# Products of zeros ahead of the first work on TensorE, three register loads moved into the first block, and a send of rows one turn earlier

## The chip, the cores and the metric

The kernel runs on one core of one Trainium2 chip. The metric is the device time of one execution in microseconds; of several runs the median is given. The five engines are TensorE (PE in the profile, its weight loads PEld), VectorE (DVE), ScalarE (ACT), GpSimd (POOL) and SyncE (SP, which issues most DMAs). Each engine executes its own instructions in order, and they wait for each other by semaphores.

## The reference

One layer of a transformer over x of 4 batches x 512 rows x 128 channels, float32:

```
x = x + LN2( attention(LN1(layernorm(x))) @ Wo )       # 16 query heads of 64, ONE key/value head
x = x + MoE(layernorm(x))
MoE: probs = softmax(x @ gate_w.T); the two best of 8 experts, shares normalised to sum 1
     for an expert: hact = up * gelu(gate), (gate, up) = x @ gate_up_w.T (512 each); out = hact @ down_w.T
```

## The kernel before

**First block, attention.** A unit is 8 heads of one batch; there are 8 units. `attention_schedule` writes one list of steps (kind, unit, number), sorted by hand-set slots, and each engine walks the same list and does its part of each step. For batch 0 the steps are: STAT0 and APPLY0 (layernorm), XT (four transposes, L1091), K (three products of split float32 operands, L1069 to L1071), Q (the same three lines, two heads at a time; ScalarE and VectorE then split the result into `q_hl`, VectorE at L974), MAX (one product per 128 queries of a head, L1121, and VectorE's row maximum, L985), SHIFT (the maxima transposed, L1128, copied by ScalarE, and sent by DMA into row 64 of `q_hm`), EXP (two products into `s_ps`, L1150 and L1152, and ScalarE's exp), V (twelve small products, L1069 to L1071), PV (L1166), SUM (L741), and NORM and OUT per head pair. For the first 12 MAX steps the slots lie ahead of the first EXP. The chain is long there: TensorE waits for layernorm, for the split of x on ScalarE and VectorE, for the split of the query weights on GpSimd (`wql`, L870), and for every second row maximum.

While batches 1 to 3 are in attention, the steps AFTER_STEPS of the batch before run in between: second layernorms, the routing (CHOOSE), PLACE, and LIST, which writes into `tile_at` which expert each tile of 128 rows has and where its rows begin. Rows are sent to their places in `sorted_rows` by indirect DMAs on GpSimd (`send_rows`, L464), eight for a batch.

**Second block, experts.** There are 39 tiles. The turn of tile k is on TensorE: turn_in(k+1) (a transpose, L1450), the register load of tile k's expert number (L1499), gate(k) and up(k) (L1461 in plain float32 for the first six tiles, L1462 to L1464 for the others), turn_hidden(k-1) (L1473), down(k-2) (L1486). ScalarE does the gelu and copies, VectorE the product of up and gelu (L1336) and `weigh` (L1345), GpSimd sends each tile's weighted rows to `parts` (L1299). The block opens with tiles 0 to 2 written out by hand: `turn_in(0)`, three register loads, eight waits for the weights of the experts, `gate(0)`, `up(0)`, and then the last unit's NORM and OUT steps in between. In this stretch ScalarE makes the high parts `wh` of the weights (L1382), and VectorE and GpSimd the low parts `wl` (L1256). GpSimd starts the block with the eight row sends of batch 2, then makes eight pieces of `wl`, then the power of the last batch's layernorm (L441). The steps of the last batch are spread over the turns by the table `BETWEEN` (PLACE in turn 9, LIST3 in turn 12). Its eight row sends follow from turn `SEND_AT` on, two, one, two, one, two per turn; while they last, GpSimd sends no results. GpSimd begins turn k once `weigh(k-3)` is done. Tiles 17 to 38 are loaded by SyncE once the last list is written and all rows are sent. The results are read back and added at the end.

## Time and profile before

| | us |
|---|---|
| median of 3 runs (lowest, highest) | 633.98 (633.31, 635.54) |
| the profiled execution: its time | 634.79 |
| its span from first to last instruction | 633.0 |
| TensorE busy | 575.8 (91%) |
| VectorE, ScalarE, GpSimd busy | 422.4, 303.7, 391.3 |

The sums that follow are made on the profiled execution's clock, on which 1.8 us lie around the span. Times of rows are from the start of the span. The matmul records' ends are modelled and reach into the next matmul, so the distance from start to start tells the rate.

### The profile page before, as it was taken

How to read it: one execution, taken by the hardware profiler on the slowest of the kernel's cores; microseconds unless marked ns; L12 is line 12 of the kernel's file. 1: busy time of each engine (PE TensorE's matmuls, PEld its weight loads, DVE VectorE, ACT ScalarE, POOL GpSimd, SP SyncE). 2: the span in 40 equal slices, each digit the busy share in tenths (PEclk: the TensorE clock that was granted, in tenths of full speed). 3: DMA queues.
4: the chain of work that ended last, by engine and by line, in shares of the span. 5: the costliest groups of instructions: out<-in, count | busy, mean ns of one | idle time of the engine just before them, and what ended most of it. 6: DMA issues, size and time to landing. Idle time of an engine off the chain costs nothing. (4 is left out here: it accounts for less than half of the span.)

```text
span 633.0 us, 8708 instructions
## 1 busy us (share of the span) xinstructions
PE 575.8 (91%) x2559; PEld 324.4 (51%) x2559; DVE 422.4 (67%) x815; ACT 303.7 (48%) x570; POOL 391.3 (62%) x319
## 2 busy tenths in 40 slices
PE   2799999999999999979999989899997989899990
PEld 1354454444554454445544544444442567788880
DVE  3777558658847978686587767977485868344433
ACT  2235655445545554354556434355544654455540
POOL 4338686658668855598597556959755934355330
PEclk9889999999999999789999978999998999999995
DMA  6121011010101100061000000000006200231005
GB/s 173 47 88 69 2 68 69 0 69 0 70 16 53 69 1 1 5 250 47 1 1 1 2 1 15 17 6 0 10 1 167 64 22 27 53 97 36 21 14 199
DMA packets 23980, 29.28 MB, mean 46 GB/s; under 512 B 4403, under 2 KB 14901, under 8 KB 23936
## 3 DMA queue, kind: packets, MB, share of 16 engines
q1 hardware_dynamic: 21664, 24.50, 11.9%
q0 software_dynamic: 2272, 4.24, 2.0%
q8 instruction: 23, 0.38, 0.3%
q14 instruction: 21, 0.17, 0.1%
HBM read 13.73 MB, written 15.32 MB: 46 GB/s over the span
## 5 line engine op out<-in xcount | busy, mean ns | idle before, releaser
L1059 ACT ACTIVATE prob<-s_ps 128x512 f32<-128x512 f32 x256 | 150.6, 598 | 191.5 <-PE s_ps L1152 189.5
L985 DVE TENSOR_REDUCE rowmax<-max_ps 128x1 f32<-128x512 f32 x256 | 173.1, 685 | 90.1 <-PE max_ps L1121 88.4
L922 POOL TENSOR_TENSOR fold<-prob 128x1024 f32<-128x1024 f32 x63 | 149.6, 2374 | 96.7 <-ACT prob L1059 96.2
L1166 PE MATMUL pv_ps<-prob,v 128*64 128x512 f32 x512 | 140.4, 628 | 0.0
L1150 PE MATMUL s_ps<-q_hl,khh 128*128 128x512 f32 x256 | 119.3, 466 | 1.5 <-DMA q_hm<-mrow 0.9
L1121 PE MATMUL max_ps<-khh,q_hl 128*128 128x512 f32 x256 | 106.0, 422 | 9.0 <-DVE q_hl L974 4.4
L1152 PE MATMUL s_ps<-q_hm,kly 65*128 65x512 f32 x256 | 102.9, 402 | 0.0
L1150 PEld LDWEIGHTS s_ps<-q_hl,khh 128*128 128x128 f32 x256 | 49.3, 193 | 81.7 <-ACT prob L1059 58.1
L928 POOL TENSOR_TENSOR psums<-fold 128x512 f32<-128x512 f32 x63 | 81.3, 1290 | 4.9
L1121 PEld LDWEIGHTS max_ps<-khh,q_hl 128*128 128x128 f32 x256 | 50.4, 197 | 30.0 <-DVE rowmax L985 10.4
L1152 PEld LDWEIGHTS s_ps<-q_hm,kly 65*128 65x128 f32 x256 | 49.4, 193 | 9.1 <-issue 3.3
L1166 PEld LDWEIGHTS pv_ps<-prob,v 128*64 128x64 f32 x512 | 25.8, 137 | 46.5 <-issue 35.3
L974 DVE TENSOR_TENSOR q_hl<-q_ps,q_hl 64x512 fp32r<-64x512 f32 x64 | 44.1, 689 | 6.5 <-ACT q_hl L1041 5.2
L1336 DVE TENSOR_TENSOR ha<-up_ps,gl 128x512 f32<-128x512 f32 x39 | 26.9, 690 | 30.6 <-PE up_ps L1464 23.5
L464 POOL DMA_INDIRECT sorted_rows<-xr,place_i x32 | 32.6, 1020 | 23.5 <-issue 11.9
L1486 PE MATMUL sum_ps<-wd,ht 128*128 x312 | 41.8, 277 | 2.6 <-DVE raw L1345 2.4
L907 POOL TENSOR_SCALAR q_hm<-q_hl 64x1024 fp32r<-64x1024 f32 x32 | 33.3, 1039 | 12.5 <-ACT q_hl L1041 12.5
L1041 ACT ACTIVATE q_hl<-q_ps 64x512 fp32r<-64x512 f32 x64 | 37.6, 587 | 6.5 <-PE q_ps L1071 5.7
L1299 POOL DMA_INDIRECT parts<-raw,psums x22 | 21.3, 970 | 30.4 <-DVE raw L1345 27.7
L1486 PEld LDWEIGHTS sum_ps<-wd,ht 128*128 128x128 f32 x312 | 37.9, 192 | 3.8 <-issue 3.8
L709 DVE TENSOR_TENSOR ao<-sum_ps,raw 128x512 f32<-128x512 f32 x32 | 22.0, 688 | 21.7 <-PE sum_ps L751 21.6
L761 PE MATMUL y_ps<-ao,wof 128*128 128x512 f32 x64 | 34.8, 628 | 0.0
(218 smaller groups left out, 769.9 us busy)
## 6 DMA issues: line engine op xcount, KB each, us to landing
sorted_rows<-raw_w SPq DMA_DIRECT2D x36, 260.0 KB, 2.6
raw_w<-in_gate_upT SPq DMA_DIRECT2D x8, 512.0 KB, 7.6
wd<-in_downT SPq DMA_DIRECT2D x8, 256.0 KB, 4.2
raw_w<-parts SPq DMA_DIRECT2D x8, 256.0 KB, 4.0
psums<-sorted_rows SPq DMA_DIRECT2D x22, 65.0 KB, 1.8
x<-in_x SPq DMA_DIRECT2D x4, 256.0 KB, 5.3
out<-x SPq DMA_DIRECT2D x4, 256.0 KB, 2.7
xs_first<-sorted_rows SPq DMA_DIRECT2D x15, 65.0 KB, 1.9
```

The source lines that it names most:

```text
L761: nc.tensor.matmul(y_ps[:, :], wof[:, c, :], ao[:, k % 2, :], start=c == 0, stop=c == PAIRS - 1).then_inc(out_mm, 1)
L922: nc.gpsimd.tensor_tensor(fold[:, :, :], prob[:, head % 4, 0:2, :], prob[:, head % 4, 2:4, :], ALU.add).then_inc(prob_folded, 1)
L928: nc.gpsimd.tensor_tensor(psums[:, head % SUM_SLOTS, :], fold[:, 0, :], fold[:, 1, :], ALU.add).then_inc(head_sum, 1)
L974: nc.vector.tensor_tensor(q_hl[DH:P, h % Q_SLOTS, :], q_ps[DH * hd:DH * hd + DH, :], q_hl[0:DH, h % Q_SLOTS, :].bitcast(F32), ALU.subtract ...
L985: nc.vector.tensor_reduce(rowmax[:, group % 2, it, i:i + 1], max_ps[:, k % 2, :], AX_X, ALU.max).then_inc(max_done, 1)
L1041: nc.scalar.activation(q_hl[0:DH, (2 * k + hd) % Q_SLOTS, :], q_ps[DH * hd:DH * hd + DH, :], ACT.Copy).then_inc(q_hi, 1)
L1059: nc.scalar.activation(prob[:, head % 4, jt, :], s_ps[:, k % 2, :], ACT.Exp, scale=SCALE).then_inc(exp_done, 1)
L1121: nc.tensor.matmul(max_ps[:, k % 2, :], q_hl[:, k // JT % Q_SLOTS, it * P:(it + 1) * P], khh[:, b % 2, :], start=True, stop=True).then_inc ...
L1150: nc.tensor.matmul(s_ps[:, k % 2, :], khh[:, b % 2, keys], q_hl[:, slot, :], start=True, stop=False)
L1152: nc.tensor.matmul(s_ps[:, k % 2, :], kly[0:DH + 1, b % 2, keys], q_hm[0:DH + 1, slot, :], start=False, stop=True).then_inc(score_mm, 1)
L1166: last = nc.tensor.matmul(pv_ps[DH * hd:DH * hd + DH, :], v[:, b % 2, jt, :], prob[:, head % 4, jt, :], start=(jt == 0), stop=(jt == JT - 1))
L1486: last = nc.tensor.matmul(down_ps[:, :], ht[:, k % 2, c * P:(c + 1) * P], wd[:, weights(k, DN, c * P, P)], start=c == 0, stop=c == FC - 1)
```

## The change

It has three parts. (1) TensorE multiplies a tile of zeros (`idle_rows`, slot 9 of `q_hm`, cleared by GpSimd at the start) into `y_ps`, which nothing reads: 20 times ahead of everything, 8 times ahead of K, 5 ahead of the first MAX, once ahead of each of MAX 2 to 11, 3 times ahead of the first EXP and 3 ahead of V. (2) The three register loads of tiles 0 to 2 stand in the first block, ahead of the last SUM. (3) `SEND_AT` is 9 where it was 10, so that the last batch's row sends begin in the turn of PLACE.

```diff
+BUSY = {"start": 20, "K": 8, "MAX": 5, "EXP": 3, "V": 3, "rows": 1}
+OPEN = 3
...
+        idle_set = sem("idle_set")
...
+        tile_expert = []
+        def load_expert(pe, k):
+            tile_expert.append(pe.value_load(tile_at[0:1, 0, k:k + 1], min_val=0, max_val=E - 1))
...
+            idle_rows = q_hm[:, Q_SLOTS - 1, :]
...
             def _(pool):
+                nc.gpsimd.memset(idle_rows.bitcast(F32), 0.0).then_inc(idle_set, 1)
                 nc.gpsimd.memset(minus_half[:, :], -0.5).then_inc(half_set, 1)
...
+                def keep_busy(times):
+                    for _ in range(times):
+                        nc.tensor.matmul(y_ps[:, :], idle_rows[:, 0:P], idle_rows, start=True, stop=True)
+                pe.wait_ge(idle_set, 1)
+                keep_busy(BUSY["start"])
                 pe.wait_ge(consts_in, 96)
                 in_bank = None
                 for kind, u, a in steps:
                     b = u // 2
+                    if u == 0 and a == 0 and kind in BUSY:
+                        keep_busy(BUSY[kind])
...
                         if it == 0:
                             pe.wait_ge(q_lo, u * UH + i + 1)
+                        if 2 <= k < 12:
+                            keep_busy(BUSY["rows"])
                         if k >= 2:
                             pe.wait_ge(max_done, k - 1)
...
+                    if (kind, u, a) == ("SUM", last_unit, 1):
+                        pe.wait_ge(tiles_ready, 1)
+                        for k in range(OPEN):
+                            load_expert(pe, k)
                     tail_tensor(pe, kind, u, a)
...
-            SEND_AT = 10
+            SEND_AT = 9
...
-            assert SEND_AT > BETWEEN["PLACE"] and EOW >= TOP_K * TPB + 4
+            assert SEND_AT >= BETWEEN["PLACE"] and EOW >= TOP_K * TPB + 4
...
-                tile_expert = []
                 turn_in(0)
-                for k in range(OPEN):
-                    expert(k)
```

How TensorE's first instructions stand, before and then with the change (the lines of the changed kernel lie 18 to 33 lines further down; L1102 is a product of zeros):

```order
L1091 MATMUL q_ps<-ident,x 128x128 [waits xn_ready,consts_in]
L1091 MATMUL q_ps<-ident,x 128x128 x3
L1069 MATMUL pv_ps<-xh,wkh 128x512 [waits wkv_split,xl_ready]
L1070 MATMUL pv_ps<-xh,wkl 128x512
L1071 MATMUL pv_ps<-xl,wkh 128x512
L1069 MATMUL q_ps<-xh,wqh 128x512 [waits xl_ready,wq_split,xnT_sb]
```

```order
L1102 MATMUL y_ps<-q_hm 128x512 [waits idle_set]
L1102 MATMUL y_ps<-q_hm 128x512 x19
L1119 MATMUL q_ps<-ident,x 128x128 [waits xn_ready,consts_in]
L1119 MATMUL q_ps<-ident,x 128x128 x3
L1102 MATMUL y_ps<-q_hm 128x512 x8
L1087 MATMUL pv_ps<-xh,wkh 128x512 [waits wkv_split,xl_ready]
L1088 MATMUL pv_ps<-xh,wkl 128x512
L1089 MATMUL pv_ps<-xl,wkh 128x512
L1087 MATMUL q_ps<-xh,wqh 128x512 [waits xl_ready,wq_split,xnT_sb]
L1088 MATMUL q_ps<-xh,wql 128x512
L1089 MATMUL q_ps<-xl,wqh 128x512
L1102 MATMUL y_ps<-q_hm 128x512 x5
```

The products of zeros stand ahead of the waits, so they run while the awaited data is made.

TensorE from the last PV of the first block over the block's end (the branches) to the first gate, before and then with the change; TENSOR_LOAD reads a register from `tile_at`:

```order
L1166 MATMUL pv_ps<-prob,v 64x512 [waits exp_done]
L1166 MATMUL pv_ps<-prob,v 64x512
L741 MATMUL sum_ps<-psums,sumsel 32x512 [waits vec_sum,head_sum]
L741 MATMUL sum_ps<-psums,sumsel 32x512 x3
L770 UNCONDITIONAL_BRANCH
L1438 UNCONDITIONAL_BRANCH [waits barrier_Pool_Activation_PE_DVE_SP_release]
L1450 MATMUL pv_ps<-ident,xs_early 128x128 [waits xs_in0,raw_ready]
L1499 TENSOR_LOAD tile_at
L1499 ISA x2
```

```order
L1196 MATMUL pv_ps<-prob,v 64x512 [waits exp_done]
L1196 MATMUL pv_ps<-prob,v 64x512
L661 TENSOR_LOAD tile_at [waits tiles_ready]
L661 ISA x2
L661 TENSOR_LOAD tile_at
L661 ISA x2
L661 TENSOR_LOAD tile_at
L661 ISA x2
L755 MATMUL sum_ps<-psums,sumsel 32x512 [waits vec_sum,head_sum]
L755 MATMUL sum_ps<-psums,sumsel 32x512 x3
L784 UNCONDITIONAL_BRANCH
```

The loads, three before as after, moved from behind the first transpose of the second block to ahead of the last SUM of the first.

GpSimd in turns 9 to 14, before and then with the change (L457 and L465 write the rows' ids, L464 and L472 send rows, L1299 and L1332 send results):

```order
L457 COPY xr<-ids 128x8 [waits rows_sent,eow_ready]
L1299 DMA parts<-raw,xs_first 4096x128 [waits x3_copied,eow_ready,place_ready,pool_own]
L464 DMA sorted_rows<-xr,place_i 18432x130 [waits eow_ready]
L464 DMA sorted_rows<-xr,place_i 18432x130
L464 DMA sorted_rows<-xr,place_i 18432x130 [waits eow_ready] x2
L464 DMA sorted_rows<-xr,place_i 18432x130
L464 DMA sorted_rows<-xr,place_i 18432x130 [waits eow_ready] x2
```

```order
L465 COPY xr<-ids 128x8 [waits rows_sent,eow_ready]
L472 DMA sorted_rows<-xr,place_i 18432x130 [waits x3_copied,place_ready,pool_own]
L472 DMA sorted_rows<-xr,place_i 18432x130
L472 DMA sorted_rows<-xr,place_i 18432x130 [waits eow_ready] x2
L472 DMA sorted_rows<-xr,place_i 18432x130
L472 DMA sorted_rows<-xr,place_i 18432x130 [waits eow_ready] x2
L472 DMA sorted_rows<-xr,place_i 18432x130
L1332 DMA parts<-raw,xs_first 4096x128 [waits eow_ready] x11
```

One send of results went from ahead of the eight row sends to behind them, and each row send waits for the `weigh` of one tile less.

## Rows read from the trace of the kernel before

**Rows 1.** The page of the profile, part 2 (40 equal slices): the granted clock.

```profile
PEclk9889999999999999789999978999998999999995
```

**Rows 2.** Windows: start:end, length, each engine's busy us, granted clock, DMA share, GB/s.

```profile
25.10:28.50 3.40, 3.19 (x9) 1.97 (x10) 2.52 (x5) 0.59 (x1) 0.00 (x0) 0.50 0.00 0
42.10:45.50 3.40, 3.40 (x9) 1.04 (x8) 1.29 (x2) 0.60 (x1) 0.00 (x0) 0.51 0.00 0
0.00:42.10 42.10, 24.00 (x78) 14.52 (x79) 25.85 (x44) 13.79 (x24) 17.30 (x33) 0.96 0.36 116
482.50:485.90 3.40, 3.28 (x4) 1.40 (x5) 1.21 (x2) 0.00 (x0) 2.78 (x3) 0.50 0.81 230
```

**Rows 3.** Timeline, TensorE, 8 to 31 us: start, us, engine, line, operation, idle before.

```profile
8.74 1.09 PE L1091 MATMUL q_ps<-ident,x 128*128 128x128 f32 x4 [8.74 <-ACT x L360]
...
12.57 0.80 PE L1069 MATMUL pv_ps<-xh,wkh 128*128 128x512 f32 x1 [2.74 <-DVE xl L963]
...
19.07 0.63 PE L1069 MATMUL q_ps<-xh,wqh 128*128 128x512 f32 x1
19.50 0.63 PE L1070 MATMUL q_ps<-xh,wql 128*128 128x512 f32 x1
...
28.63 0.39 PE L1070 MATMUL q_ps<-xh,wql 128*128 128x512 f32 x1
28.86 0.40 PE L1071 MATMUL q_ps<-xl,wqh 128*128 128x512 f32 x1
...
30.15 0.47 PE L1150 MATMUL s_ps<-q_hl,khh 128*128 128x512 f32 x1 [0.90 <-DMA q_hm<-mrow]
```

**Rows 4.** Timeline, GpSimd and VectorE, 12 to 32 us.

```profile
12.06 1.58 POOL L870 TENSOR_TENSOR wql<-prob,wqh 128x512 fp32r<-128x512 f32 x1
...
29.91 1.41 DVE L974 TENSOR_TENSOR q_hl<-q_ps,q_hl 64x512 fp32r<-64x512 f32 x2 [0.71 <-ACT q_hl L1041]
```

**Rows 5.** Timeline, TensorE, at the value projection of the first batch.

```profile
40.09 0.30 PE L1069 MATMUL q_ps<-wvh,xh 128*128 128x64 f32 x1 [0.94 <-DVE q_hl L974]
```

**Rows 6.** Timeline, ScalarE and TensorE, around the end of the first block.

```profile
475.04 0.60 ACT L1059 ACTIVATE prob<-s_ps 128x512 f32<-128x512 f32 x1 [1.02 <-PE s_ps L1152]
...
477.66 1.06 PE L741 MATMUL sum_ps<-psums,sumsel 128*32 128x512 f32 x8
...
482.62 2.07 PE L1461 MATMUL gate_ps<-raw_w,xe 128*128 x2 [2.52 <-issue]
...
486.04 0.27 PE L1450 MATMUL pv_ps<-ident,xs_early 128*128 128x128 f32 x1
```

**Rows 7.** Line L1499, TensorE's sequencer: ns min/median/max, first and last start.

```profile
L1499 PEldq TENSOR_LOAD <-tile_at x3: 311/312/489, 479.8 to 481.4; - x3
...
L1499 PEldq TENSOR_LOAD <-tile_at x1: 303/303/303, 549.4 to 549.4; - x1
```

**Rows 8.** Timeline, GpSimd and VectorE, 490 to 507 us.

```profile
490.69 1.41 POOL L1256 TENSOR_TENSOR wl<-raw_w,wh 128x512 fp32r<-128x512 f32 x1 [0.83 <-ACT wh L1382]
...
503.98 1.04 POOL L441 TENSOR_TENSOR rstd<-var_eps,minus_half 128x4 f32<-128x4 f32 x1 [0.18 <-DVE var_eps L480]
...
506.02 1.13 DVE L500 SCALAR_TENSOR_TENSOR x<-z,rstd,x 128x128 f32<-128x128 f32 x4
```

**Rows 9.** Timeline, all engines, 528 to 549 us.

```profile
528.66 0.98 POOL L1299 DMA_INDIRECT parts<-raw,xs_first  x1 [3.50 <-DVE raw L1345]
...
536.56 0.34 DVE L1345 TENSOR_SCALAR raw<-sum_ps,xs_first 128x128 f32<-128x128 f32 x1
...
542.14 0.97 POOL L464 DMA_INDIRECT sorted_rows<-xr,place_i  x1 [0.30 <-issue]
...
544.28 1.06 PE L1486 MATMUL sum_ps<-wd,ht 128*128 x8
...
547.23 0.30 PE L1450 MATMUL pv_ps<-ident,psums 128*128 128x128 f32 x1 [1.89 <-DMA psums<-sorted_rows]
...
548.11 0.49 PE L1462 MATMUL gate_ps<-wh,xeh 128*128 x1 [0.58 <-issue]
```

More of the change, by code:

```diff
@@ L1215, in bass_preln_mqa_moe_kernel @@
             parts_in = [sem(f"parts_in{b}") for b in range(NB)]
-            OPEN = 3
             BETWEEN = {"YT": 3, "YSTAT": 3, "YADD": 4, "XSTAT": 4, "XNORM": 5, "X3T": 6, "LOGIT": 6, "CHOOSE0": 6, "CHOOSE1": 7,
@@ L1495, in between_step @@
                     after_tensor(pe, kind, LB, bank)
-                def expert(k):
-                    tile_expert.append(pe.value_load(tile_at[0:1, 0, k:k + 1], min_val=0, max_val=E - 1))
                 def gate(k):
@@ L1550, in _ @@
                             pe.wait_ge(tiles_ready, 2 if k < FIRST_TILES else 3)
-                        expert(k)
+                        load_expert(pe, k)
                         if k == RAW_TILES:
```

## The prediction, made before the changed kernel ran

> **What bounds the kernel now.** TensorE is busy for 575.8 of 633.0 us, so I looked first for the stretches in which it is not, or in which it works at half rate. The windows say where: up to 42.1 us it is busy for only 24.0, so 18.1 us are idle [rows 2]. The timeline of the same stretch says that work, too, is slow there: at 19 us two products of 512 columns start 0.43 us apart, at 28.6 us 0.23 apart [rows 3]. The first is the 1.2 GHz level of the clock and the second 2.4 GHz. The granted clock is not written down for the time before its first change, so the page and the windows print 1.00 there; the distances in the timeline are what counts. Two more falls to 0.50 come at 25.1 and 42.1, 3.4 us each, both behind stretches in which TensorE waited [rows 2]. From about 45 us on TensorE is the bound, and what it reaches earlier there stays. The digits of the page show later falls (slices 17 and 18, 24 and 25, 31) [rows 1]; only the last is touched by the change.
>
> The second place is the change of blocks. The last SUM starts at 477.66, and the first gate at 482.62, after 2.52 us for which nothing is named but "issue" [rows 6]; the row of line L1499 says what it is, three register loads, the first at 479.8 and the third at 481.4 [rows 7]. Gate and up then run at the clock of 0.50 [rows 2], and the next transpose starts at 486.04 [rows 6].
>
> The third is tile 17. TensorE's down product of turn 15 starts at 544.28 and ends at 545.34, the transpose of tile 17 waits 1.89 us for a DMA and starts at 547.23, and the gate only at 548.11, because the register load stands behind the transpose [rows 9].
>
> **Part 1, zeros at the start.** Added are one clearing on GpSimd (about 0.5 us at a time when it waits for statistics) and 49 products. At half rate they are 49 x 0.43 = 21 us, at full rate 49 x 0.23 = 11 us, against 18.1 us of idle time [rows 2, 3], so the clock decides. The 20 opening ones start near 1.4 us; at full rate throughout they end at 6.0, at half rate at 10.0. I take the middle, 8, for a clock that rises among them; the transposes could start at 8.74 before [rows 3], so nothing is lost, and 1.3 is if it does not rise.
>
> What the chain up to the first score product at 30.15 [rows 3] then saves, each at full instead of half rate: the four transposes 1.09 to about 0.6, 0.5; K's three products 3 x 0.20 = 0.6, of which 0.3 is lost, since Q must wait for GpSimd's `wql`, which ends at 13.64 [rows 4]; the first Q 0.6; the second Q 0.6; the transposes of SHIFT about 0.45; and five MAX products that stand alone between two row maxima, 0.80 each before as the lone product at 12.57, 0.47 as the lone one at 30.15 [rows 3], 1.5 in all (estimate from these two). That is 3.95; VectorE's own pace takes some back, as its row maxima follow each other without a gap once TensorE is fast, and I take 3.4. The check is VectorE's third split at 29.91 [rows 4], which should come near 26.5. The zeros ahead of MAX and EXP lie in waits (EXP waited 0.90 for the DMA [rows 3], three zeros are 0.7).
>
> Then V: 0.94 us of waiting [rows 5], into which three zeros go (0.7). Behind it came the fall at 42.1, in which TensorE was busy throughout [rows 2]; at half rate it lost half of 3.4, 1.7. With the zeros I think the fall is avoided more often than not, but falls in between are possible too: I take 1.0, with bounds of -0.5 and 1.7. The Trainium skill, "TensorE: Matmul & The Clock Gate", Part 1, says that the default state is throttled and that activity releases the throttle; by that rule alone the zeros pay the whole 1.7, and the trace agrees in that every fall stands behind waits. Neither says that operands of zeros count as activity, which is a rival below.
>
> **Part 2, the loads.** They leave the front of the second block, but do not vanish. In the old place their starts are 0.8 us apart [rows 7], three are 2.4. In the new place they stand behind the last PV, whose wait is over when the last exp ends, at 475.64 [rows 6]. The sequencer runs ahead of the array: the load at 549.4 is one of a turn whose gate comes more than one us later and costs nothing [rows 7, 9]. So loads run from 475.7 to 478.1, and SUM starts there and not at 477.66: 0.4 later. If the sequencer could not run ahead, they would start as the PV products end, at 477.7, and cost 2.4. I take 0.4, by the nearer row. The Trainium skill, "DMA: Bandwidth & Descriptors", table of latencies, gives about 0.6 us as the floor of such a load; by it three end at 477.5 and SUM is not delayed; the row shows 0.8, and the row decides.
>
> Everything of the second block moves with SUM, by 0.4 later. What does its front gain? The gate starts some 2.0 earlier (of the 2.52, part is the waits for the weights, which stay), and if the clock then holds, gate and up take 2.0 and not 3.4: 3.5 in all by the transpose at 486.04, 2.0 if it falls again. But TensorE is not alone here. GpSimd has eight sends first and then eight pieces of `wl` until 503.8, and only then the power of the layernorm at 503.98 [rows 8]. Its slack is what counts: it waited 0.83 for ScalarE at 490.69, of which 0.6 can go; 0.18 at 503.98; and its power ended at 505.02, 1.0 before VectorE used it at 506.02 [rows 8]. So VectorE comes there at most 0.6 + 0.18 + 1.0 = 1.8 earlier, and the split of tile 6, the product of tile 5 and `weigh(2)` are queued behind it on VectorE, which TensorE's down(3) waits for. Gain of part 2: the smaller of 1.8 and the front, less 0.4, is 1.4.
>
> **Part 3, the row sends.** A send and the idle time after it are 0.97 + 0.30 = 1.27. The first goes where a send of results stood, 528.66. The last two now wait for `weigh` of tile 10, over at 536.90, and not of tile 11; with about 0.8 to the issue (estimate) the last is issued at 539.0 instead of 542.14. From that issue to the transpose of tile 17 were 5.1 us [rows 9], so its rows are there at 544.1, 1.1 before they are due at 545.2. The wait goes wholly, and the load behind it hides again: 548.11 - 545.3 = 2.8. Moved past it is one send of results; `eow` has 16 buffers and no more than six results are behind, so nothing waits for it.
>
> **The sum.** 3.4 + 1.0 + 1.4 + 2.8 = 8.6, from 634.79: 626.2. The profiled execution is 0.8 above the median of the runs, so by the median it could be 625.4; I say 626.0.
>
> **Rivals.** (a) *The clock falls once more among the zeros.* Between the eight zeros ahead of K and the first MAX, TensorE works for K and Q only, and GpSimd's 13.64 [rows 4] holds it. A fall there or in V costs 1.7 and more of the chain: the start gives 2.0 and not 4.4, 628.6. For it: the falls at 25.1 and 42.1 came behind waits of the same size. (b) *GpSimd does not bind in the second block*: its pieces of `wl` may get shorter when VectorE's move away from them. Then the front's 3.5 - 0.4 remain, 624.5. (c) *The loads wait for the array*: 2.0 more, 628.2. (d) *The row sends do not free tile 17*, because the list or a send comes later than I think: 2.8 less, 629.0. This is also the case that part 3 does not do what it says. (e) *Zeros do not raise the clock*, and lie on the path at 0.43 each. Price: 20 from 1.4 end at 10.0 against 8.74, 1.3; 8 are 3.4 against 2.74 of waiting [rows 3], 0.7; 5 ahead of MAX 0.7; ten single ones 4.3 against some 2.7 of waits, 1.6; EXP and V 0.3 each; 4.9 in all. With parts 2 and 3 at 4.2 this ends at 635.5, slower than before; it decides from 4.2 us of uncovered zeros on. Against it: the rows before show a clock that followed how busy TensorE was, and nothing in them ties it to values; nothing in them excludes it either.
>
> **How the numbers follow.** Noise first: the three runs spread over 0.35%, and 0.3% (1.9 us) is about what can be told from no change. Chances: the forecast 0.60 (its own range 624.3 to 628), (a) 0.17, (b) 0.08, (c) 0.04, (d) 0.06, (e) 0.05. The range reaches to (a) to (d) with their spread: 623.3 to 630. All cases but (e) are faster by more than 1.9; with something for a pile-up of (a), (c) and (d), faster is 0.92, same 0.05, slower 0.03.
>
> **What the changed profile would show.** Right: products of zeros 0.23 apart before 8.7; the first score product near 26.8; clock at 1.00 from 42 to 45 of the old count; SUM 0.4 later than the last exp allows; the first gate within 2 us of the block's start; the power on GpSimd right behind its last `wl` piece with VectorE waiting for it; tile 17's transpose without a wait for DMA. Wrong: zeros 0.43 apart beyond 9 us, a fall between 9 and 30, an idle TensorE ahead of SUM of over 1 us, or a wait for `psums` rows at tile 17.

## The result, and the profile after

The changed kernel takes 628.81 us in the median of 20 executions (623.05 to 634.88), the kernel before 634.84 in the same sitting (20 executions, 631.76 to 636.23): a ratio of 0.9896 [0.9874, 0.9917]. It is 6.0 us faster, and its median lies 2.8 above the forecast of 626.0. Its executions lie much further apart than those of before, and time goes with the mean granted clock of an execution: 0.985 at 623.05, 0.965 at 634.88. Medians are over all executions; ratios leave out those more than 1.5% above the fastest of their kernel (two of the 20 here). In a later sitting the same program was measured again beside the kernel before, and the ratio was 0.9979 [0.9952, 1.0006]. The two intervals do not touch, and the second just includes no change. So the changed kernel is faster by 1.0% in one sitting and by 0.2% in the other, and the experiments below are compared by what their traces show stage by stage first, and by ratios second.

The profiled execution has a span of 629.1 (time 631.12) against 633.0. The table cuts it at five starts on TensorE: the 17th score product of a `u`, the last SUM, and the transposes that turn in tiles 6, 16 and 38.

| stage | before | after | change | forecast |
|---|---|---|---|---|
| start to the 17th score product | 58.82 | 55.46 | -3.36 | -4.4 |
| from there to the last SUM | 418.84 | 413.40 | -5.44 | +0.4 |
| SUM to tile 6's transpose | 28.90 | 36.15 | +7.25 | -1.8 |
| tile 6 to tile 16 | 35.77 | 35.77 | 0.0 | 0 |
| tile 16 to tile 38 | 65.20 | 62.32 | -2.88 | -2.8 |
| tile 38 to the end | 25.42 | 26.06 | +0.64 | 0 |

Two lines agree with the forecast and two do not at all: the attention lost 5.4 us for which no term stood in the sum, and the opening of the second block grew by 7.3 where it should have shrunk.

The granted clock of after, from the page, beside [rows 1]:

```profile
PEclk9999999999999999889999999999998799999995
```

Slices 24 and 25, around 373 us, read 7 and 8 before and read 9 now; so do the second and the third, which read 8. The windows of two falls that after has of its own (columns as in [rows 2]):

```profile
14.80:18.20 3.40, 3.40 (x9) 2.33 (x7) 1.95 (x3) 1.19 (x2) 1.84 (x3) 0.50 0.00 0
489.30:496.10 6.80, 3.45 (x10) 2.31 (x11) 6.16 (x5) 0.60 (x1) 1.61 (x2) 0.50 0.16 39
```

The start, timeline of TensorE in after, beside [rows 3]:

```profile
3.68 4.04 PE L1102 MATMUL y_ps<-q_hm 128*128 128x512 f32 x15
8.52 0.63 PE L1119 MATMUL q_ps<-ident,x 128*128 128x128 f32 x4 [0.81 <-ACT x L368]
...
12.18 0.50 PE L1087 MATMUL pv_ps<-xh,wkh 128*128 128x512 f32 x1 [1.18 <-DVE xl L981]
...
14.06 0.47 PE L1087 MATMUL q_ps<-xh,wqh 128*128 128x512 f32 x1 [0.92 <-issue]
...
14.83 2.34 PE L1102 MATMUL y_ps<-q_hm 128*128 128x512 f32 x5
...
28.50 0.47 PE L1180 MATMUL s_ps<-q_hl,khh 128*128 128x512 f32 x1 [0.36 <-DMA q_hm<-mrow]
```

The zeros do raise the clock: fifteen in 4.04 us, the four transposes in 0.63 instead of 1.09, K at the full rate. But then the clock falls: the five zeros at 14.83 take 2.34, which is a distance of 0.43, and the window above says 0.50. And the first query product starts at 14.06, no earlier than in the trace of before (14.02), because it waits for GpSimd, whose last piece of `wq` ends at 13.96, 0.3 later than in [rows 4]. The piece ahead of it took 1.06 where it took 0.62 before; VectorE's split of `x`, which is earlier now, ran beside it until 12.12. First TensorE in before, then GpSimd in after:

```profile
14.02 0.63 PE L1069 MATMUL q_ps<-xh,wqh 128*128 128x512 f32 x1
...
11.54 1.06 POOL L887 TENSOR_SCALAR wqh<-prob 128x512 fp32r<-128x512 f32 x1
12.68 1.28 POOL L888 TENSOR_TENSOR wql<-prob,wqh 128x512 fp32r<-128x512 f32 x1
```

The first score product starts 1.65 us earlier, not 3.4.

The opening of the second block, timeline of TensorE in after, beside [rows 6]:

```profile
468.86 1.06 PE L755 MATMUL sum_ps<-psums,sumsel 128*32 128x512 f32 x8 [0.25 <-issue]
470.95 0.33 PE L1483 MATMUL pv_ps<-ident,xs_early 128*128 128x128 f32 x1 [1.03 <-ACT raw L733]
471.84 1.75 PE L1494 MATMUL gate_ps<-raw_w,xe 128*128 x2 [0.56 <-ACT xe L1424]
...
475.09 0.42 PE L1483 MATMUL pv_ps<-ident,xs_early 128*128 128x128 f32 x1
```

From SUM to the second transpose it is 6.23 us, 8.38 before: the loads are gone from there, and the gain of 2.15 is there although the clock falls again. What took it back, and 7 us more, stands a little later. GpSimd, VectorE and TensorE, timelines of after:

```profile
481.05 9.87 POOL L1289 TENSOR_TENSOR wl<-raw_w,wh 128x512 fp32r<-128x512 f32 x8
...
481.73 0.69 DVE L723 TENSOR_TENSOR ao<-sum_ps,raw 128x512 f32<-128x512 f32 x1
482.34 9.65 DVE L1289 TENSOR_TENSOR wl<-raw_w,wh 128x1024 fp32r<-128x1024 f32 x1
491.92 0.68 DVE L723 TENSOR_TENSOR ao<-sum_ps,raw 128x512 f32<-128x512 f32 x1
...
492.65 2.07 PE L775 MATMUL y_ps<-ao,wof 128*128 128x512 f32 x2 [7.71 <-DVE ao L723]
```

VectorE's second piece of `wl` is recorded with 9.65 us. The same instruction took 1.30 in the kernel before, timeline of VectorE:

```profile
493.15 1.30 DVE L1256 TENSOR_TENSOR wl<-raw_w,wh 128x1024 fp32r<-128x1024 f32 x1
...
496.93 4.48 DVE L1256 TENSOR_TENSOR wl<-raw_w,wh 128x1024 fp32r<-128x1024 f32 x2 [1.26 <-ACT wh L1382]
```

So three of VectorE's four pieces ran while GpSimd's eight were under way (490.69 to 503.80) in before too; there the engines took turns.

The long piece of after ends 1.07 us after the last of GpSimd's eight pieces (490.92), which is its own work, and those eight ran back to back, 1.23 us each. VectorE was held out for the rest of a train of GpSimd's instructions. Behind the piece in its queue stood the fourth normalisation, for which TensorE waited 7.71 us, and during that wait the clock fell (0.50 from 489.3 to 496.1).

Tile 17, timeline of TensorE in after, beside [rows 9]:

```profile
542.72 1.06 PE L1519 MATMUL sum_ps<-wd,ht 128*128 x8
543.61 0.27 PE L1483 MATMUL pv_ps<-ident,psums 128*128 128x128 f32 x1
```

No wait for a DMA is left, and the turn is as long as the ones around it (2.84).

### The profile page after: what moved, and what is told of

It reads as the page before. It is cut to its first block and busy times, and to the rows that moved or that the text cites. A ratio compares the mean times of both kernels' runs of the same rounds, so it can differ in the third digit from the quotient of the medians.

```text
span 629.1 us, 8805 instructions
## 1 busy us (share of the span) xinstructions
PE 580.3 (92%) x2608; PEld 330.5 (53%) x2608; DVE 427.6 (68%) x815; ACT 304.0 (48%) x570; POOL 389.4 (62%) x320
## 5 line engine op out<-in xcount | busy, mean ns | idle before, releaser
L1196 PE MATMUL pv_ps<-prob,v 128*64 128x512 f32 x512 | 138.8, 622 | 0.0
L1151 PE MATMUL max_ps<-khh,q_hl 128*128 128x512 f32 x256 | 103.5, 410 | 6.2 <-DVE q_hl L992 3.0
L1196 PEld LDWEIGHTS pv_ps<-prob,v 128*64 128x64 f32 x512 | 25.7, 136 | 46.0 <-issue 35.4
L472 POOL DMA_INDIRECT sorted_rows<-xr,place_i x32 | 32.4, 1013 | 21.7 <-issue 12.2
L1332 POOL DMA_INDIRECT parts<-raw,psums x22 | 21.4, 972 | 30.3 <-DVE raw L1378 27.6
```

What stands on the lines that cost most here:

```text
L1151: nc.tensor.matmul(max_ps[:, k % 2, :], q_hl[:, k // JT % Q_SLOTS, it * P:(it + 1) * P], khh[:, b % 2, :], start=True, stop=True).then_inc ...
L1196: last = nc.tensor.matmul(pv_ps[DH * hd:DH * hd + DH, :], v[:, b % 2, jt, :], prob[:, head % 4, jt, :], start=(jt == 0), stop=(jt == JT - 1))
```

## The experiments

Theories. *H*: the loads bring TensorE and VectorE earlier against GpSimd, so that VectorE is held out by the eight pieces of `wl`; this costs some 8 us. Its rivals: the early reading of the numbers costs itself; or the hold-out lies beside other work. *C*: half of what the zeros should give at the start is lost to a fall of the clock among them. Its rival: the chain of the start is not TensorE's alone. And for part 3 the question is why it is worth so little by itself. The runs come from four sittings: before and after; zeros_only to pool_gaps; zeros_sends to late_low_fill; loads_wait to start_sends. The last three were on three different chips. Each table row is one profiled execution ("half clock" is the time at 0.50 between 60 and 460 us); "medians" and "ratio" come from all its executions and those of the kernel before in the same sitting.

| kernel | zeros, loads, sends | to 17th score | half clock | 17th score to SUM | SUM to tile 6 | tile 10 to 16 | tile 16 to 38 | medians, before / this | ratio |
|---|---|---|---|---|---|---|---|---|---|
| before | - - - | 58.82 | 20.4 | 418.84 | 28.90 | 19.49 | 65.20 | | |
| after | z l s | 55.46 | 10.2 | 413.40 | 36.15 | 19.60 | 62.32 | 634.84 / 628.81 | 0.9896 [0.9874, 0.9917] |
| zeros_only | z - - | 56.08 | 10.2 | 413.62 | 29.83 | 19.78 | 67.27 | 635.6 / 628.81 | 0.9888 [0.9851, 0.9925] |
| loads_only | - l - | 59.64 | 17.0 | 417.82 | 35.91 | 19.81 | 67.60 | 635.6 / 643.48 | 1.0116 [1.0093, 1.014] |
| sends_only | - - s | 59.08 | 17.0 | 416.08 | 29.71 | 22.82 | 63.06 | 635.6 / 634.73 | 0.9977 [0.9954, 1.0001] |
| pool_gaps | z l s, gaps | 55.91 | 17.0 | 417.51 | 27.29 | 21.42 | 63.20 | 635.6 / 628.67 | 0.9863 [0.9825, 0.9901] |
| zeros_sends | z - s | 57.03 | 10.2 | 414.05 | 28.59 | 19.44 | 62.27 | 634.1 / 624.4 | 0.9834 [0.9797, 0.9871] |
| wait_for_two | z l s, wait | 55.81 | 10.2 | 414.14 | 28.27 | 19.59 | 62.31 | 634.1 / 626.7 | 0.989 [0.9853, 0.9927] |
| late_low | z l s, moved | 56.34 | 0 | 410.04 | 33.50 | 19.59 | 62.32 | 634.1 / 626.77 | 0.9892 [0.9858, 0.9927] |
| late_low_fill | same, more z | 55.06 | 17.0 | 417.56 | 32.12 | 19.51 | 62.30 | 634.1 / 629.27 | 0.9917 [0.9887, 0.9947] |
| loads_wait | - l -, wait | 58.21 | 17.0 | 416.54 | 28.23 | 19.66 | 67.50 | 634.71 / 635.09 | 1.0006 [0.9979, 1.0033] |
| after_again | z l s | 55.92 | 3.4 | 410.46 | 33.01 | 22.81 | 62.62 | 634.71 / 633.21 | 0.9979 [0.9952, 1.0006] |
| sends_again | - - s | 58.13 | 17.0 | 416.08 | 29.55 | 22.66 | 63.17 | 634.71 / 632.77 | 0.9963 [0.9938, 0.9988] |
| start_sends | 20 z - s | 58.33 | 17.0 | 416.07 | 29.58 | 22.77 | 62.27 | 634.71 / 633.12 | 0.9982 [0.996, 1.0004] |

### Each part alone

zeros_only keeps `BUSY` and puts the loads and `SEND_AT = 10` back; loads_only and sends_only set

```diff
-BUSY = {"start": 20, "K": 8, "MAX": 5, "EXP": 3, "V": 3, "rows": 1}
+BUSY = {"start": 0, "rows": 0}
```

with no clearing either, and keep one of the other two parts.

> The products of zeros alone, loads and sends as before. Theory: they bring 3.4 to 4.4 us in the first block and nothing elsewhere, and since the front of the second block is as before, VectorE's second wl piece is not held out there: about 630.5, one group of times. Rival (the spread of the changed kernel's times comes from the clock in attention, not from the second block): the times spread over 8 us or more here too.

> The three register loads in the first block alone. Theory: the front of the second block is earlier, GpSimd's wl pieces then meet VectorE's second piece, which is held out through several of them in some of the runs: times in two groups, near 633 (1.4 better) and near 640 (7.7 of waiting added), and the profile shows which. Rival: the hold-out is chance of the profiled run; one group at 633.4.

> The row sends one turn earlier alone. All theories: tile 17 no longer waits, 2.8 less than before, one group near 632, no wait for DMA at tile 17's transpose.

The zeros give 6.8 us, more than the 3.4 to 4.4 expected (the rest comes in the attention, see below), and their ratio is that of the whole changed kernel. Their six executions spread over 6.9 us, though the traced one has no long piece; the mean clocks run from 0.964 to 0.982. The loads alone lose 7.9 in the median, and the six executions lie close together (641.69 to 644.72): one group and not two. One of them was traced; that the piece was held in all six is inferred from their times. Their trace has the piece of VectorE again, timelines of VectorE and GpSimd in loads_only:

```profile
489.64 9.89 POOL L1289 TENSOR_TENSOR wl<-raw_w,wh 128x512 fp32r<-128x512 f32 x8
...
490.95 9.67 DVE L1289 TENSOR_TENSOR wl<-raw_w,wh 128x1024 fp32r<-128x1024 f32 x1
```

The sends alone are worth about nothing: the 2.1 us from tile 16 to 38 come, and 3.3 are lost between tile 10 and tile 16. zeros_only shows on TensorE what part 3 is for:

```profile
540.70 0.30 PE L1478 MATMUL pv_ps<-ident,psums 128*128 128x128 f32 x1 [2.33 <-DMA psums<-sorted_rows]
```

### Taking the hold-out away

In pool_gaps GpSimd waits for its own semaphore after each piece, so that there is a moment without a piece between two.

```diff
                     last = eng.tensor_tensor(wl[:, cols], raw_w[:, cols], wh[:, cols].bitcast(F32), ALU.subtract)
+                    if pieces > 1 and n < pieces - 1:
+                        link_pool(eng, last)
                 last.then_inc(done, 1)
+                if pieces > 1:
+                    eng.wait_ge(done, e - 1)
```

> The changed kernel, but GpSimd waits for its own semaphore after each of its eight wl pieces, so that they do not run back to back. Theory (VectorE is held out because the pieces follow without a gap): VectorE's second wl piece takes at most 2.6 us, the 7.7 us wait of TensorE for ao is gone, all runs lie at 623 to 627. Rival (a piece once refused stays refused until GpSimd has nothing to do): the 9.7 us piece stays and the median with it.

In wait_for_two GpSimd starts its eight only when VectorE's first two are done; loads_wait is the same line in loads_only.

```diff
                     send_rows(i)
+                pool.wait_ge(wl_ready, 2)
                 for e in range(2, E - 2):
```

> The changed kernel, with GpSimd waiting for both of VectorE's first two pieces before its own eight. Theory (VectorE is refused only when GpSimd has a piece running and the next one ready): VectorE's pieces take 1.2 to 1.4 us each, GpSimd's eight run back to back in 9.9 us but begin 1 to 1.5 us later, SUM to the sixth turn-in 27 to 30 us, time 622 to 628. Rival (the order in which they meet doesn't matter, VectorE is held whenever GpSimd runs a train, and the last two pieces meet it too): one of the pieces at the end takes over 5 us and the time stays at 628 to 631.

> The loads alone (no zeros, sends in turn 10), with GpSimd waiting for VectorE's first two pieces before its own eight. Theory (the 7.9 us that the loads alone lost are the refused piece and nothing else): no piece of VectorE over 2.5 us, SUM to the sixth turn-in 28 to 29 us instead of 35.9, time 633.5 to 636.5 against 643.48 for the loads alone, so the same as before within 0.3%. Rival (reading the numbers early itself costs): 640 to 644, with the loss in another place.

In all three the long piece is gone. VectorE and GpSimd, timelines of loads_wait:

```profile
488.25 1.22 DVE L1289 TENSOR_TENSOR wl<-raw_w,wh 128x1024 fp32r<-128x1024 f32 x1
...
492.27 4.38 DVE L1289 TENSOR_TENSOR wl<-raw_w,wh 128x1024 fp32r<-128x1024 f32 x2 [1.48 <-ACT wh L1416]
...
489.55 11.97 POOL L1289 TENSOR_TENSOR wl<-raw_w,wh 128x512 fp32r<-128x512 f32 x8 [2.61 <-DVE wl L1289]
```

The two engines still meet, but each waits for one piece of the other: VectorE's last two take 2.15 and 2.30, two of GpSimd's 2.29. SUM to tile 6 falls from 35.91 to 28.23, by 7.7, and the median from 643.48 to 635.09, with ratios of 1.0116 and 1.0006 that lie far apart. This settles the larger part of H: the loss is the held piece, and one wait on GpSimd, with the loads where they were, gives the 7.9 us back. The rival that reading early itself costs so much is out. Two of the twelve executions of loads_wait, though, took 640.35 and 642.37, the other ten 632.46 to 637.03, and their mean clocks (0.965 and 0.960) are no lower than those of some of the ten. Neither was traced. So the wait is not shown to prevent the hold-out every time; the last two pieces of VectorE still meet the train. What H says of the cause, that coming earlier is what lets a piece be held, is shown only as a difference between programs, since pieces met the train before as well.

It is as plain that the loads give nothing in return. loads_wait is no different from before (1.0006 [0.9979, 1.0033]), and wait_for_two hardly from zeros_sends in the stage (28.27 and 28.59); its ratio is the higher one, with intervals that just overlap. Where the gain goes shows on TensorE and VectorE in wait_for_two:

```profile
496.70 1.07 POOL L449 TENSOR_TENSOR rstd<-var_eps,minus_half 128x4 f32<-128x4 f32 x1
...
494.26 1.31 DVE L490 TENSOR_SCALAR neg_mean<-moments 128x4 f32<-128x4 f32 x1
...
497.24 1.15 PE L1520 MATMUL sum_ps<-wd,ht 128*128 x8 [0.92 <-DVE raw L1379]
```

The power of the layernorm stands right behind the last piece of `wl` with no idle time: GpSimd binds, as the forecast had it. In pool_gaps VectorE waits for that power:

```profile
500.53 1.14 DVE L508 SCALAR_TENSOR_TENSOR x<-z,rstd,x 128x128 f32<-128x128 f32 x4 [0.30 <-POOL rstd L449]
```

The wait in wait_for_two put GpSimd's train some 2.65 us later, counted from SUM, and with it went what the front had won. pool_gaps, where GpSimd starts at once and VectorE is let in, has the shortest stage of all, 27.29, which is 1.6 under before: there, and only there, the forecast gain of 1.8 (less 0.4 at SUM) can be seen. Its median is above what was expected; its traced execution lost time in two other places that its row names: 17.0 us at half clock in the attention, and 21.42 from tile 10 to 16.

### The loads undone, the rest kept

```diff
-                    if (kind, u, a) == ("SUM", last_unit, 1):
-
-                        pe.wait_ge(tiles_ready, 1)
-                        for k in range(OPEN):
-                            load_expert(pe, k)
 ...
                 turn_in(0)
+                for k in range(OPEN):
+                    load_expert(pe, k)
```

> The changed kernel without its second part: the zeros and the sends in turn 9 stay, the three experts' numbers are read in the second block again. Theory (the loads gain about 1.4 to 2 us at the block's opening and give back about 8 us through the refused second piece of VectorE): no piece of VectorE over 2.5 us, SUM to the sixth turn-in 28.5 to 30 us instead of 36.15, and a time of 621.5 to 626, below the changed kernel's 628.8. Rival (the sends' part is worth nothing and the hold-out lies beside other work): 627 to 630, the same as the zeros alone (628.81).

This is the best kernel of the study, 624.4, 9.7 us under before (0.9834 [0.9797, 0.9871]), in all six executions below 625.6. It was measured in a sitting without the standstill that is told below. The two engines meet as they did before; timelines of VectorE and GpSimd in zeros_sends:

```profile
486.24 1.29 DVE L1284 TENSOR_TENSOR wl<-raw_w,wh 128x1024 fp32r<-128x1024 f32 x1
...
483.78 13.08 POOL L1284 TENSOR_TENSOR wl<-raw_w,wh 128x512 fp32r<-128x512 f32 x8 [0.48 <-ACT wh L1410]
```

The part of the change that costs is part 2: by the stage 7.6 us in after and 4.4 in after_again, by the ratios 0.6% against the first sitting of the changed kernel (0.9896) and more against the second, in which 3.2 us are the standstill in turn 12 (22.81 and 19.60 from tile 10 to 16).

### Moving the piece, and filling more of the start

late_low moves VectorE's second piece; late_low_fill has more zeros on top of that.

```diff
                 tail_vector(dve, "NORM", last_unit, 2)
-                low_gate_up(dve, 1, wl_ready)
                 tail_vector(dve, "NORM", last_unit, 3)
                 hidden(2)
+                low_gate_up(dve, 1, wl_ready)
 ...
-BUSY = {"start": 20, "K": 8, "MAX": 5, "EXP": 3, "V": 3, "rows": 1}
+BUSY = {"start": 20, "K": 14, "Q": 5, "MAX": 5, "EXP": 3, "V": 3, "rows": 1}
```

> The changed kernel with VectorE's second piece moved behind its fourth normalisation and its third hidden product, so that a piece refused for long holds up neither. Theory: if a piece is refused, it is now one that the weights' later experts need and not the attention's output, and SUM to the sixth turn-in is 27 to 29 us; time 621 to 626, the lowest of the kernels that keep all three parts. Rival (the place of the piece is not what costs; TensorE needs the low halves themselves that early): SUM to the sixth turn-in stays over 32 us, time 628 to 632.

> late_low with 14 zeros instead of 8 ahead of the key product and 5 new ones ahead of the first query product, where TensorE's row still shows gaps between 10 and 14 us. Theory of the missed half of part 1 (the fall of the clock in the first 26 us takes the second half of the start's gain): with the gaps filled the clock doesn't fall between 14 and 26 us, the first EXP starts at 26.5 to 27.5 instead of 28.50, and the time is 1 to 2 us below late_low. Rival (the fall comes whatever the zeros do, it only moves): first EXP at 28 to 29 again, and the same time as late_low within 1 us.

VectorE is held out here too, and moving the piece saves 2.65 of the 36.15 only, not the 7 to 9 expected; the rival's number came, over 32, but not for its reason. Timeline of VectorE in late_low:

```profile
480.73 11.99 DVE L1289 TENSOR_TENSOR wl<-raw_w,wh 128x1024 fp32r<-128x1024 f32 x3
492.65 0.34 DVE L1378 TENSOR_SCALAR raw<-sum_ps,xs_early 128x128 f32<-128x128 f32 x1
```

The attention's output is through, but now `weigh(0)` is queued behind the held piece, and TensorE's down product for it. In each of the three positions in which a piece was held (after, late_low, after_again) something that TensorE needs was queued behind it.

The filled start answers C. The window from 5.00 to 28.10 us of late_low_fill has no fall (PEclk 1.00 with the clock already at its higher level), and still the first score starts at 28.10:

```profile
5.00:28.10 23.10, 19.48 (x82) 13.36 (x81) 13.52 (x20) 6.83 (x13) 11.49 (x24) 1.00 0.34 104
```

Its timelines of TensorE and VectorE:

```profile
14.28 0.39 PE L1087 MATMUL q_ps<-xh,wqh 128*128 128x512 f32 x1
...
28.10 0.47 PE L1180 MATMUL s_ps<-q_hl,khh 128*128 128x512 f32 x1 [0.37 <-DMA q_hm<-mrow]
...
20.40 1.41 DVE L992 TENSOR_TENSOR q_hl<-q_ps,q_hl 64x512 fp32r<-64x512 f32 x2
21.84 3.85 DVE L1003 TENSOR_REDUCE rowmax<-max_ps 128x1 f32<-128x512 f32 x6
25.89 1.29 DVE L1003 TENSOR_REDUCE rowmax<-max_ps 128x1 f32<-128x512 f32 x2 [0.20 <-PE max_ps L1151]
27.70 1.41 DVE L992 TENSOR_TENSOR q_hl<-q_ps,q_hl 64x512 fp32r<-64x512 f32 x2 [0.52 <-ACT q_hl L1059]
```

VectorE runs from 20.4 to 25.7 without a gap, six row maxima 0.64 apart. With the clock never down, the start gives 2.05 us and not 3.4: the rest was VectorE's and GpSimd's to give. The fall among the zeros costs the other 0.4 of after. So both halves of C are needed, and the rival has the larger one: the 26.5 to 27.5 that C expected did not come, the rival's 28 to 29 did. In time the filled kernel is not faster (629.27 against 626.77); of the two traced executions its own had 17.0 us at half clock in the attention and that of late_low none.

### Again, and the opening zeros alone

after_again and sends_again are the changed kernel and sends_only unchanged. start_sends is zeros_sends with

```diff
+BUSY = {"start": 20, "K": 0, "MAX": 0, "EXP": 0, "V": 0, "rows": 0}
```

> The changed kernel once more. If the hold-out is in the program's order and not in chance, VectorE's second piece takes 9.5 to 9.8 us again and SUM to the sixth turn-in is 35.5 to 36.5. Rival (the meeting within 0.05 us is chance): a piece of 1.2 to 2.4 us in this execution, SUM to the sixth turn-in 28 to 30. Either way the time lies between 623 and 632.

> The sends in turn 9 alone, once more. If the wait of about 2 us ahead of the down product in turn 12 belongs to this program, turn-in 10 to turn-in 16 takes 22.5 to 23 us again; rival (it is chance of one execution, as the changed kernel's own 19.6 suggests): 19.4 to 19.9. Time 631 to 636.

> The zeros of the start alone (20 of them), with the sends in turn 9 and no early loads: the zeros ahead of the key product, the maxima, the scores and the value product are gone. Theory (the start's zeros give the full clock to the first turn and products, and it falls again in the gaps before 26 us; the zeros ahead of V keep the clock up at 42 us): the clock is half between 13 and 20 us, the first EXP starts at 29.5 to 30.2, another fall comes at 38 to 44 us, and the time is 627 to 631, some 3 to 5 us above the one with all zeros (624.4). Rival (the first 20 do all the work): first EXP at 28.2 to 28.8 and 623 to 626.

after_again is held out again, but it is another piece, the first of VectorE's last two. Timelines of GpSimd, VectorE and TensorE:

```profile
480.36 9.92 POOL L1289 TENSOR_TENSOR wl<-raw_w,wh 128x512 fp32r<-128x512 f32 x8
...
482.06 10.43 DVE L1289 TENSOR_TENSOR wl<-raw_w,wh 128x1024 fp32r<-128x1024 f32 x2 [1.25 <-ACT wh L1415]
...
493.00 2.07 PE L1519 MATMUL sum_ps<-wd,ht 128*128 x8 [5.62 <-DVE raw L1378]
```

It started 0.46 us into a piece of GpSimd's, not 0.05 as in after, so nearness is not what decides; my expectation had both outcomes and neither of its times for the stage (33.01 is between them), and the median of 633.21 is above the 623 to 632 that I gave. The stage is shorter than in after because the held piece is one behind which only `weigh(0)` waits. Over all traces: with the loads early and GpSimd free to start, VectorE is held out in 5 of 5 (after, after_again, loads_only, late_low, late_low_fill); in the other nine in none.

sends_again repeats sends_only within 0.2 us in each stage behind the 17th score product (up to it, it is 0.95 shorter), with the loss ahead of the down product of turn 12. Its timelines of TensorE and VectorE:

```profile
533.88 1.15 PE L1514 MATMUL sum_ps<-wd,ht 128*128 x8 [2.13 <-DVE raw L1373]
...
531.29 0.18 DVE L642 TENSOR_TENSOR tile_j<-tile_j,begun 128x22 f32<-128x22 f32 x1
533.28 0.35 DVE L1373 TENSOR_SCALAR raw<-sum_ps,xs_first 128x128 f32<-128x128 f32 x1 [1.81 <-remote]
```

VectorE stands still for 1.8 us between two of its own instructions, and a fall of the clock follows at 535.6. It is not VectorE's alone. ScalarE waits 2.34 in the same trace and starts again at the same time, and between 531.80 and 532.80 no instruction runs on TensorE, VectorE or ScalarE (timeline of ScalarE and window of sends_again):

```profile
532.89 0.28 ACT L1419 ACTIVATE xeh<-pv_ps 128x128 fp32r<-128x128 f32 x1 [2.34 <-remote]
...
531.80:532.80 1.00, 0.00 (x0) 0.00 (x0) 0.00 (x0) 0.00 (x0) 0.03 (x1) 1.00 0.21 67
```

The same stage is as long in start_sends and after_again (22.77 and 22.81), a little shorter in pool_gaps, and long in none of the others. All five have the sends in turn 9, but so have five traces without it, the first one of the changed kernel among them. The sittings divide them: all five with the standstill are of the second and the fourth sitting, all five without it of the first and the third. The three traces of the second and fourth that have the sends in turn 10 have a small form of it: updates 1.6 to 1.8 late, a wait of ScalarE of 0.96 to 0.99, and a stage that is hardly longer (19.66 to 19.81, against 19.44 to 19.60 where no update is late). So it goes with the sitting, and the early sends make it long. What differs between the sittings is open; their traces also hold fewer semaphore updates (5037 to 5118, against 5837 to 5845), so that the recording itself may have a part in it. It follows that sends_only and sends_again say what part 3 is worth by itself in those two sittings only.

start_sends is the surprise among the zeros. The twenty at the start raise the clock, then it falls at 13.8 and stays down to 30.9; window of start_sends:

```profile
13.90:30.90 17.00, 12.63 (x26) 6.67 (x27) 11.26 (x17) 3.50 (x6) 4.46 (x13) 0.50 0.04 14
```

Its first score starts at 30.71, later than the 30.15 of [rows 3] and than the theory had it, and its median is that of sends_again (633.12 and 632.77). The fall between 38 and 44 us that the theory expected without zeros ahead of V did not come. Twenty of the 49 zeros are worth nothing without the other 29, which sit in the gaps: what they buy is not the rise but that it lasts. Which of the 29 are needed was not tried.

## Why the prediction was right, and where it was not

**The start.** That zeros raise the clock and none of them lies on the path was right, and rival (e) is out. Of the chain's 3.4, 1.65 came. The step that failed is "VectorE's own pace takes some back", which I sized at 0.55; late_low_fill puts it at 1.9 (3.95 - 2.05). Part of it is the first query product, for which I had only half of K's gain lost to GpSimd's `wql`: GpSimd's split came 0.3 us later than before. The five MAX products were summed a little low as well, 5 x 0.33 is 1.65 and not 1.5, which makes the miss larger by 0.15. The remaining 0.4 is rival (a): a fall between 14 and 26 us is in seven of the eight traces with all zeros, and missing only in the filled one.

**V.** The fall at 42.1 is in none of the eight traces with all zeros. From the first score product to the 17th it is 26.96 in after and 28.67 before: 1.7, the upper bound, where I took 1.0. (In loads_wait, sends_again and start_sends, without zeros ahead of V, there is no fall there either, and it is 27.97, 27.60 and 27.62; so 0.7 to 1.1 of the 1.7 go with that fall, and zeros are not the only way to be without it.) Start and V together: 3.36 in after, 2.75 in the mean of eight traces with all zeros against the six without (55.95 and 58.70), where I had 4.4 and rival (a) 2.0. By that mean, rival (a) is the nearer.

**What the sum lacked.** The attention. I wrote that the later falls are not touched. Over the fourteen traces the stage from the 17th score to SUM is 416.1 to 418.8 in the six without all zeros and 410.0 to 417.6 in the eight with them, and it follows the half-clock column: 418.8 at 20.4 us, 413.4 to 414.1 at 10.2, 410.0 at none. The means are 416.9 and 413.8, so the traces with the zeros of the first 40 us are 3.1 us shorter there on the average, hundreds of us later. That is the greater part of why after came near the forecast at all, and it fits the 12 us over which its executions spread: the two profiled ones of the same program had 10.2 and 3.4 us at half clock there. That the full set of zeros goes with fewer falls is shown; how the first 40 us reach that far is not. The waits behind which these falls stand did not go away: TensorE waits some 1.5, 2 to 3.2, 1.5 and 1.6 us in all fourteen traces, near 250, 275, 368 and 390 us. Before has a fall behind the first three, late_low behind none. The first of them on TensorE, in before and in late_low:

```profile
252.21 0.50 PE L1121 MATMUL max_ps<-khh,q_hl 128*128 128x512 f32 x1 [1.55 <-DVE q_hl L974]
...
249.73 0.50 PE L1151 MATMUL max_ps<-khh,q_hl 128*128 128x512 f32 x1 [1.53 <-DVE q_hl L992]
```

So a wait of the same length can be followed by a fall or not, and the forecast, which put this term at nothing, had no reason to.

**The loads.** The 0.4 at SUM was right: from the last score product to SUM it is 3.69 to 3.86 in the traces with loads there and 3.38 in those without, so rival (c) is out. The front too: 2.15 by the second transpose with a fall of the clock (I had 2.0), 3.6 without (late_low, after_again: 4.80 against 8.38; I had 3.5). GpSimd as the binding engine was right as well, by pool_gaps. The step that failed is taking "its pieces of `wl`" as a fixed row of work that costs VectorE nothing more when it comes closer: with VectorE 2 us earlier one of its pieces took 9.65. Its pieces lay inside the train before too and took turns there, so it is not the overlap itself that is new. The term was -1.4 and measured +7.25 (+7.7 in loads_only against loads_wait). The Trainium skill, "SBUF — State Buffer", section "SBUF: two separate sides", says that VectorE and GpSimd share a lock that one of them holds for a whole instruction, the other being blocked meanwhile. The traces agree for one piece (2.15 to 2.4 us where 1.2 is usual). That one engine was passed over up to seven times in a row is what the traces add; no run here shows that the lock is what did it.

**The sends.** 2.8 forecast, 2.88 measured, and the wait at tile 17 is gone in every trace with them. In sends_only 2.1 come there and 3.3 are lost to the standstill in turn 12, which neither the forecast nor a rival had; the ratios 0.9977 and 0.9963 are what is left. Beside zeros_only the sends are worth more, 5.0 from tile 16 to 38 (67.27 and 62.27): in the three other traces without them (zeros_only, loads_only, loads_wait) the rows are waited for 2.3 to 2.4 us, 1.89 before, and the clock falls right behind that wait, which it does not in before.

The median lay within the range for reasons that partly cancel: against the forecast the profiled execution is 1.0 worse at the start, 9.1 worse in part 2's stage and 0.6 at the end, and 5.8 better in the attention, which makes 3.8 us gained for 8.6.

## What to carry to other kernels

- Before an engine is brought earlier, look at what it will then run beside. Two engines whose pieces had taken turns at the cost of one piece each met 2 us earlier, and one was held out for the rest of the other's train. A wait that starts the train behind VectorE's first two pieces costs 2.65 us of start and saved 7.7 in the trace, though two of twelve executions took some 6 us more than the rest even so.
- A part that is right by its own row (2.15 us at the front) can be the one that makes the change worse: leaving part 2 out gives 0.9834 in one sitting, where all three give 0.9896 and 0.9979 in two others. Measure parts of a change alone and in pairs.
- Where the time of an execution follows the granted clock, a few runs of one program say less than its traces stage by stage: the same kernel gave 0.9896 and 0.9979 in two sittings. A kernel whose parts are compared should have them all in one sitting; here they were not, and the standstill in turn 12 came in two of the four.

## What the runs showed of the hardware

- VectorE was passed over while GpSimd began four (late_low_fill, 7.29 us) to seven (late_low, 9.73 us) further instructions, in 5 traces. In others the two took turns piece by piece. In loads_only the held piece was 9.67 us against 1.2 to 2.3 in loads_wait. What decides was not found: the start of the held piece was 0.02 to 0.06 us from the start of one of GpSimd's in four traces, and 0.46 behind it in the fifth.
- Products of zeros count as activity for the clock: it rose at 4.3 to 6.9 us in nine traces, with nothing but zeros running on TensorE until then. A group of 20 alone did not keep it: 0.50 from 13.9 to 30.9.
- Three register loads ahead of SUM cost it 0.3 to 0.5 us; in their old place, with the array idle, taking them away gave 2.15.
- Fewer falls of the clock in the attention, at 250 to 374 us, go with zeros that end at 40 us: 0 to 17.0 us at half clock against 17.0 to 20.4. The waits there are as long with zeros as without (1.53 and 1.55 us at the first).
- In five traces the updates of TensorE's semaphores came 1.1 to 3.3 us behind the recorded ends of its products in one turn (sends_again: 532.83 for 529.81), and VectorE and ScalarE stood still until then.
